# Down product of a gated block: the last eight of sixteen units as block products in two groups of four

## The chip, the cores and the metric

One NeuronCore of a Trainium2 chip runs the whole kernel. The metric is the device time of one execution in microseconds. Engines: TensorE (PE; PEld is its weight load), VectorE (DVE), ScalarE (ACT), GpSimd (POOL) and SyncE (SP), whose queue issues every DMA.

## The reference, cut to what matters

```
x = x + tanh(g_xattn) * attention(layernorm(x), ctx)        # x: 4 batches x 512 rows x 512
x = x + tanh(g_ffn) * ffn(layernorm(x))
ffn(x): up = x @ wu.T; gate = x @ wg.T                      # 2048 hidden, weights rounded to -1, 0, 1 times a scale
        hidden = silu(up) * gate
        return hidden @ wd.T
```

The change lies in the last line, `hidden @ wd.T`.

## The kernel before, in words

**Units.** The up and gate products are made in 16 units n: eight pairs of 128-wide blocks of the hidden dimension, for batches 0 and 1 (n = 0 to 7), and again for batches 2 and 3 (n = 8 to 15). In a unit the two batches and the two hidden blocks form a 2 x 2 scheme, and seven products (Strassen's, in Winograd's form) stand for eight: `product1` to `product7`, of 8 matmuls with 512 columns each (a high and a low f16 part of x, L692 and L694). Products 1, 6, 7 and 4 gather in `ps_c[n % 2]`, product 2 in `ps_y`, products 5 and 3 in `ps_z`. ScalarE copies partial results out (`copy_1`, `copy_5`, `copy_u2`), VectorE adds the others (`add_11`, `add_12`, `add_22`), and each waits for the other.

**Hidden parts.** A unit leaves four hidden blocks "11", "12", "21", "22" of 128 x 512: first index the hidden block, second the batch. ScalarE makes the SiLU (L1027), VectorE multiplies by the gate (`make_h`, L1342), ScalarE rounds to a high f16 part (`high_h`, L1033), VectorE subtracts for the low part (`low_h`, L1347).

**Down product.** For units 0 to 11 (`down_half`, L770): during unit n = 3 to 14 one down half stands between product 3 and product 7. It takes two finished units and one batch, 4 row tiles x 8 matmuls with 512 columns (L764), two PSUM halves in turn, and VectorE adds each tile to its rows (`evict`, L1382). For units 12 to 15 the down product is itself done by seven block products (`final`, L796 to L847) over 256-column halves: they need sums S1 to S4 of the hidden blocks (GpSimd L553 to L573, VectorE for unit 15 at L1466; high parts `high_s`, L1039; low parts `low_s`, L551 and L1352) and sums T1 to T4 of the down weights (GpSimd, L539 to L544). Parts 1, 6, 7, 4 and 5, 3 add up in their banks, so a part waits for the eviction of the one before. This is the kernel's tail, 224 matmuls of 256 columns (L806), evicted at L1395.

**Order.** Each engine's order is written out by hand and waits on semaphores. TensorE in unit n (L783): product 6, product 3, the down half, product 7, then products 1, 2 and 5 of unit n + 1, then product 4 of n. Product 6 waits for `copy_1`, product 3 for `copy_5`, product 7 for `copy_u2`, product 4 for `add_22`, product 2 and 5 of the next unit for `add_11` and `add_12`. ScalarE's queue is at L1102, VectorE's at L1400, GpSimd's at L531 to L573.

**Reload.** Rows of batches 0 and 1 are stored during units 9 and 10, and the rows of batches 2 and 3 are read back into the same buffer (L422); `shift` (L1073) adds a term to them on ScalarE.

Of the kernel before, what the change touches and what calls it, by code (L numbers as in the profile page):

```python
# [6 lines left out]
def gated_block_kernel(nc, x, xT, first, ctxT, wqkT, wugT, wdT, x1_dram, out):  # L7

# [35 lines left out]
    with stack:  # L44
# [109 lines left out]
        LAST_D = NN - 4  # L154
        FIN = [(j, t) for j in (1, 6, 5, 7, 2, 3, 4) for t in range(NT)]
# [88 lines left out]
        def sum_part(n, c, lo):  # L244

            if c == "S1":
                return h_part(n, "12", lo)
            k = ((n - LAST_D) * 3 + SUMS.index(c) - 1) * 2 + lo
            for home, size in ((xt_flat, 8), (xf[:, 6144:8192], 8), (t3_flat, 4), (early, 4)):
                if k < size:  # L250
                    return home[:, k * 256:(k + 1) * 256].bitcast(F16)
                k -= size

        def hidden(n, c, lo):
            return h_part(n, c, lo) if c in HSLOT else sum_part(n, c, lo)

        def hidden_ready(n, c):
            return (s_lo[c], n + 1) if c in HSLOT else (s_slo[c], n - LAST_D + 1)

        def last_td(r, c):  # L260

            view = t_d[:, 8 * DM:16 * DM].rearrange("p (u r c n) -> p u r c n", u=4, r=2, c=2)
            return view[:, :, r, c, :]

        def last_t(blk):

            m, u = {"T1": (0, 0), "T2": (0, 4), "T3": (1, 0), "T4": (1, 4)}[blk]
            units = wbf[:, m, :].rearrange("p (u c) -> p u c", u=NU)
            return units[:, u:u + 4, A21 * 256:(A21 + 1) * 256]

        def fin_done(j, t):

            return FIN.index((j, t)) + 1

        def fin_bank(j, t):

            if j in (1, 6, 7, 4):
# [23 lines left out]
        def _(sp):  # L301
# [122 lines left out]
            for b, t, j in ((2, 0, 3), (2, 1, 3), (2, 2, 3), (2, 3, 3), (3, 0, 4), (3, 1, 4), (3, 2, 4)):  # L424
                sp.wait_ge(s_ef, fin_done(j, t))
                sp.dma_start(out[b, t * P:(t + 1) * P, :], y_tile(b, t)).then_inc(d_out, 16)
            for c in (1, 0):
                sp.wait_ge(s_ef, fin_done((4, 7)[c], 3))
# [6 lines left out]
        def _(pool):  # L435
# [100 lines left out]
            hold(pool, s_tda, 3)  # L536
            hold(pool, d_tb["T3"], d_tb_done(NU, "T3"))
            hold(pool, s_sum, 4 * NU)
            pool.tensor_tensor(last_t("T1"), last_td(0, 1), last_td(0, 0), ALU.subtract).then_inc(s_tw, 1)  # L539
            pool.tensor_tensor(last_t("T3"), last_td(1, 1), last_td(0, 1), ALU.subtract).then_inc(s_tw, 1)  # L540
            hold(pool, s_tw, 1)
            pool.tensor_tensor(last_t("T2"), last_td(1, 1), last_t("T1"), ALU.subtract).then_inc(s_tw, 1)
            hold(pool, s_tw, 3)
            pool.tensor_tensor(last_t("T4"), last_td(1, 0), last_t("T2"), ALU.subtract).then_inc(s_tw, 1)  # L544
# [4 lines left out]
            def low_s(n, c):  # L549
                hold(pool, s_shi[c], n - LAST_D + 1)  # L550
                pool.tensor_tensor(sum_part(n, c, 1), sum_f32(c), sum_part(n, c, 0), ALU.subtract).then_inc(s_slo[c], 1)  # L551

            for k in range(3):  # L553
                n = LAST_D + k
# [18 lines left out]
                low_s(n, "S4")  # L573


        @block.tensor
        def _(pe):
# [120 lines left out]
            def product1(n):  # L698
# [11 lines left out]
                if n >= 4:  # L710
                    pe.wait_ge(s_ev, 4 * min(n - 3, LAST_D))
# [71 lines left out]
            for n in range(NN - 1):  # L783
# [9 lines left out]
            n = NN - 1  # L793
            ends = (NN - 4, NN - 3, NN - 2)

            def final(j, t, units, first, last):  # L796

                c, w = OPERAND[j], WEIGHT[j]
                if t == 0:
                    ready, count = hidden_ready(units[-1], c)  # L800
                    pe.wait_ge(ready, count)
                for u in units:
                    cols = last_t(w)[:, u - LAST_D, :] if j >= 4 else last_td(*w)[:, u - LAST_D, :] if j < 3 else \
                        last_td(1, 1)[:, u - LAST_D, :]
# [742 lines left out]
```

## Time and profile before

| | |
|---|---|
| median of 3 runs | 403.47 us (402.99 to 403.74) |
| the profiled execution | 402.79 us |
| its span, first to last instruction | 401.0 us |
| TensorE / VectorE / ScalarE / GpSimd busy | 395.7 / 295.3 / 261.2 / 127.0 us |
| TensorE clock granted, mean | 0.999 |

A row of a timeline is: start, duration, engine, line, operation, output and input, count, and in brackets the idle time before it and who ended it. A matmul's duration is its latency: matmuls follow each other sooner than that, so distances between starts are read. A row of a group is: line, engine, operation, forms, count, busy us, mean ns of one, idle time before.

### The profile page before, as it was taken

What the parts mean: (1) busy time and instruction counts of PE and PEld (TensorE: products, weight loads), DVE (VectorE), ACT (ScalarE), POOL (GpSimd) and SP (SyncE); (2) the same over time, 40 slices, a digit from 0 to 9 for tenths busy, and PEclk for the clock granted to TensorE, in tenths of its full rate; (3) what the DMA queues carried; (4) which work ended last, traced back from release to release, by engine and by line L of the source; (5) the groups of instructions that cost most, each with busy time, mean ns of one, the idle gap of its engine ahead of it and who ended that gap; (6) DMA issues with size and microseconds to landing.
All of it is one profiled execution on the core that took longest, in us unless ns stands there. A gap on an engine that the chain in (4) does not pass through costs nothing.

```text
span 401.0 us, 5690 instructions
## 1 busy us (share of the span) xinstructions
PE 395.7 (99%) x1816; PEld 197.6 (49%) x1816; DVE 295.3 (74%) x431; ACT 261.2 (65%) x349; POOL 127.0 (32%) x169
## 2 busy tenths in 40 slices
PE   8999999999999999999999999999999999999996
PEld 6545555454444444444444444444444444444785
DVE  0576578988899984879798877656565657595985
ACT  3886898889767786769788855733534556627510
POOL 0234254658865013313246004500000152525100
PEclk9999999999999999999999999999999999999999
DMA  8999939498600020020009533051400000000005
GB/s 306 412 418 401 386 117 235 137 284 188 159 0 3 0 105 2 0 106 0 1 16 226 111 65 60 26 183 54 158 0 2 0 2 1 0 2 1 2 2 209
DMA packets 42029, 43.89 MB, mean 109 GB/s; under 512 B 30864, under 2 KB 31120, under 8 KB 39952
## 3 DMA queue, kind: packets, MB, share of 16 engines
q1 hardware_dynamic: 42000, 43.53, 34.4%
q8 instruction: 15, 0.25, 0.2%
q14 instruction: 14, 0.11, 0.1%
HBM read 29.89 MB, written 6.29 MB: 90 GB/s over the span
## 4 chain that ended last, share of the span: by engine, by line
PE 82%; DVE 6%; ACT 5%; issue 4%; DMA 2%; SPq 1%; DVEq 0%; POOL 0%; ACTq 0%; POOLq 0%
PE pair L692 20%; PE pair L694 20%; PE pair L764 20%; PE pair L621 8%; PE pair L806 6%; PE pair L596 3%; PE pair L582 3%; DMA xf<-in_wdT 2%; PE pair L607 1%; ACT xf L1027 1%; ACT sh L1033 1%; DVE sh L1347 1%; DVE x_sb L1218 1%; PE pair L632 1%; DVE small L1223 1%
## 5 line engine op out<-in xcount | busy, mean ns | idle before, releaser
L692 PE MATMUL pair<-xb_hi,w_sb 128*128 128x512 f16 x448 | 169.8, 379 | 0.6 <-ACT xf L1071 0.3
L694 PE MATMUL pair<-xb_lo,w_sb 128*128 128x512 f16 x448 | 169.8, 379 | 0.0
L764 PE MATMUL pair<-x_sb,sh 128*128 128x512 bf16 x384 | 85.3, 379 | 0.3 <-DVE x_sb L1382 0.3
L692 PEld LDWEIGHTS pair<-xb_hi,w_sb 128*128 128x128 bf16 x448 | 43.8, 98 | 55.1 <-issue 1.5
L694 PEld LDWEIGHTS pair<-xb_lo,w_sb 128*128 128x128 bf16 x448 | 43.8, 98 | 52.3 <-issue 0.3
L1027 ACT ACTIVATE xf<-xf,small 128x512 f32<-128x512 f32 x48 | 34.6, 721 | 53.0 <-DVE xf L1337 31.2
L764 PEld LDWEIGHTS pair<-x_sb,sh 128*128 128x128 f16 x384 | 37.3, 98 | 46.5 <-DVE x_sb L1382 1.8
L621 PE MATMUL pair<-sh,xt_sb 128*128 128x512 f32 (+2 forms) x160 | 57.4, 508 | 0.0
L1342 DVE SCALAR_TENSOR_TENSOR xf<-xf,small 128x512 f32<-128x512 f32 x48 | 39.3, 821 | 12.2 <-ACT xf L1027 12.2
L1382 DVE SCALAR_TENSOR_TENSOR x_sb<-pair,small,x_sb 128x512 f32<-128x512 f32 x48 | 35.9, 747 | 13.4 <-PE pair L764 13.2
L621 PEld LDWEIGHTS pair<-sh,xt_sb 128*128 128x128 f32 x160 | 28.0, 190 | 26.2 <-issue 22.0
L1347 DVE TENSOR_TENSOR sh<-xf,sh 128x512 f16<-128x512 f32 x44 | 37.5, 858 | 0.4 <-ACT sh L1033 0.3
L1033 ACT ACTIVATE sh<-xf 128x512 f16<-128x512 f32 x44 | 27.1, 624 | 16.4 <-PE pair L764 10.7
L478 POOL TENSOR_TENSOR w_sb<-w_sb 128x512 bf16<-128x512 bf16 x8 | 9.6, 1196 | 65.2 <-ACT w_sb L899 65.2
L1332 DVE TENSOR_TENSOR xf<-pair,xf 128x1024 f32<-128x1024 f32 x16 | 19.6, 1222 | 13.8 <-PE pair L694 13.8
L1342 DVE SCALAR_TENSOR_TENSOR c<-c,small,pair 128x512 f32<-128x512 f32 x16 | 11.9, 745 | 18.2 <-ACT c L1027 18.2
L1059 ACT ACTIVATE xf<-pair 128x1024 f32<-128x1024 f32 x16 | 16.4, 1023 | 11.5 <-PE pair L694 11.3
L1327 DVE TENSOR_TENSOR xf<-pair,xf 128x1024 f32<-128x1024 f32 x16 | 19.5, 1221 | 4.9 <-PE pair L694 4.3
L558 POOL TENSOR_TENSOR xf<-xf 128x512 f32<-128x512 f32 x3 | 3.8, 1266 | 61.0 <-DVE xf L1342 61.0
L1337 DVE TENSOR_TENSOR xf<-pair,xf 128x1024 f32<-128x1024 f32 x16 | 19.5, 1220 | 3.9 <-PE pair L694 3.8
L1218 DVE SCALAR_TENSOR_TENSOR x_sb<-pair,small,x_sb 128x512 f32<-128x512 f32 x16 | 12.0, 747 | 11.8 <-PE pair L621 11.8
L893 ACT ACTIVATE w_sb<-w_sb,small 128x1024 f32<-128x1024 f32 x16 | 18.9, 1229 | 0.0
(151 smaller groups left out, 538.6 us busy)
## 6 DMA issues: line engine op xcount, KB each, us to landing
w_sb<-in_wugT SPq DMA_DIRECT2D x8, 1024.0 KB, 10.6
xt_sb<-in_xT SPq DMA_DIRECT2D x16, 256.0 KB, 5.1
x_sb<-in_x SPq DMA_DIRECT2D x4, 1024.0 KB, 9.5
xf<-in_wdT SPq DMA_DIRECT2D x4, 1024.0 KB, 6.4
xt_sb<-in_wdT SPq DMA_DIRECT2D x4, 1024.0 KB, 5.2
out<-x_sb SPq DMA_DIRECT2D x15, 256.0 KB, 2.0
x_dram<-x_sb SPq DMA_DIRECT2D x8, 256.0 KB, 2.8
x_sb<-x_dram SPq DMA_DIRECT2D x2, 1024.0 KB, 5.6
```

The source lines that it names most:

```text
L621: last = pe.matmul(ps_x[i % 2][:, lo:hi], xt_tile(i)[:, k, :], at[:, k, lo:hi], start=(k == 0), stop=(k == KD - 1))
L692: pe.matmul(dst[:, m * 512:(m + 1) * 512], w[:, o:o + P], hi[:, k], start=start and k == 0, stop=False, skip_group_check=not start)
L694: last = pe.matmul(dst[:, m * 512:(m + 1) * 512], w[:, o:o + P], lo[:, k], start=False, stop=k == 1, skip_group_check=not start)
L764: ins = pe.matmul(dst, h_part(n, c, lo)[:, i * P:(i + 1) * P], t_d[:, e * DM + lo_col:e * DM + hi_col], start=first and n == units[0] and ...
L806: ins = pe.matmul(fin_bank(j, t), hidden(u, c, lo)[:, t * P:(t + 1) * P], cols, start=first and u == units[0] and lo == 0 and (t % 2 == 0 ...
L1027: act.activation(cb(n, c)[:, 0:512], src, ACT.Silu, scale=su[:, :]).then_inc(s_silu[c], 1)
L1033: act.activation(h_part(n, c, 0), cb(n, c)[:, 0:512], ACT.Copy).then_inc(s_hi[c], 1)
L1327: dve.tensor_tensor(cb(n, "11"), ps_y[:, :], cb(n, "11"), ALU.add).then_inc(s_c["11"], 1)
L1332: dve.tensor_tensor(cb(n, "12"), ps_z[:, :], cb(n, "12"), ALU.add).then_inc(s_c["12"], 1)
L1342: dve.scalar_tensor_tensor(cb(n, c)[:, 0:512], cb(n, c)[:, 0:512], kap[:, :], gate, ALU.mult, ALU.mult).then_inc(s_mul[c], 1)
L1347: dve.tensor_tensor(h_part(n, c, 1), cb(n, c)[:, 0:512], h_part(n, c, 0), ALU.subtract)\
L1382: dve.scalar_tensor_tensor(y_tile(b, i), at, c_out[:, :], y_tile(b, i), ALU.mult, ALU.add)\
```

## The change

Units 8 to 11 are taken out of the down halves and become a first group (g = 0) of block products; units 12 to 15 stay the second group (g = 1).

- TensorE: down halves stand only in units 3 to 10. In each of units 12 to 15, row tile t = n - 12 of group 0 is worked off: seven parts (`between`) of 8 matmuls with 256 columns stand between the seven products, in two banks of the `ps_c` that the unit doesn't use. Unit 11 has no down work; its order is products 6, 3, 7, then 2 of unit 12, 4, then 1 and 5 of unit 12.
- The order of products in units 13 to 15 is 2, 5, 1, two parts, 6, 3, two parts, 7, two parts, 4, one part. In the tail the parts with block 1 of all four units stand in one piece.
- Sums S1 to S4 with high and low parts are now made for units 8 to 15. "12" has no part of its own from unit 8 on. New places for them: the weight units that are no longer read (`freed`) and, for units 14 and 15, the columns of the tile that is already used.
- GpSimd: T sums for both groups, two after unit 8, two after unit 9, two after unit 12, two after unit 13. It waits for all transposes of the second half before its first S3.
- ScalarE: the shifts of batches 2 and 3 go from units 12 and 13 to units 11 to 14, one tile of each; `sign_down(3)` stands a little earlier in unit 8. The queues of ScalarE and VectorE for units 11 to 15 are written anew.

The core of the diff:

```diff
-        LAST_D = NN - 4
-        FIN = [(j, t) for j in (1, 6, 5, 7, 2, 3, 4) for t in range(NT)]
+        G0, G1 = NU, NU + 4
+        PART = (1, 5, 6, 3, 7, 2, 4)
+        FIN = [(0, j, t) for t in range(NT) for j in PART] + [(1, j, t) for j in (1, 6, 5, 7, 2, 3, 4) for t in range(NT)]
...
+            if g == 0:
+                o = 0 if j in (1, 6, 7, 4) else 512
+                return ps_c[(t + 1) % 2][:, o:o + 256]
...
+                if n == G0:
+                    hold(pool, s_tda, 3)
+                    hold(pool, s_p[4], G0 + 1)
+                    weights_1(0)
+                if n == G0 + 1:
+                    weights_2(0)
+                if n == G1:
+                    hold(pool, s_p[4], G0 + 2)
+                    weights_1(1)
+                if n == G1 + 1:
+                    weights_2(1)
...
-            for n in range(NN - 1):
+            for n in range(G1 - 1):
                 product6(n)
                 product3(n)
                 if n >= 3:
                     down_half(n)
...
+            def between(n, j):
+
+                t = n - G1
+                if j in (1, 5):
+                    pe.wait_ge(s_mul["21"], n)
+                else:
+                    pe.wait_ge(s_ef, fin_done(0, {6: 1, 7: 6, 4: 7, 3: 5, 2: 3}[j], t))
+                final(0, j, t, group, j in (1, 5, 2), True)
+
+            n = G1 - 1
             product6(n)
             product3(n)
             product7(n)
...
+            product2(n + 1)
             product4(n)
+            product1(n + 1)
+            product5(n + 1)
+            for n in range(G1, NN):
+                if n == G1:
+                    product6(n)
+                    between(n, 1)
+                    product3(n)
+                    between(n, 5)
+                    between(n, 6)
+                    product7(n)
+                    between(n, 3)
+                else:
+                    product2(n)
+                    product5(n)
+                    product1(n)
+                    between(n, 1)
+                    between(n, 5)
+                    product6(n)
+                    product3(n)
+                    between(n, 6)
+                    between(n, 3)
+                    product7(n)
+                between(n, 7)
+                if n == G1:
+                    product4(n)
+                    between(n, 2)
+                else:
+                    between(n, 2)
+                    product4(n)
+                between(n, 4)
...
+            n = G1 - 1
+            silu(n - 1, "21")
+            copy_u2(n)
+            high_s(n - 1, "S1")
+            high_s(n - 1, "S2")
+            high_h(n - 1, "21")
+            silu(n, "12")
+            high_h(n, "11")
+            high_s(n - 1, "S4")
+            silu(n, "22")
+            high_s(n, "S3")
+            high_h(n, "22")
+            silu(n, "21")
+            copy_1(n + 1)
+            high_s(n, "S1")
+            high_s(n, "S2")
+            copy_5(n + 1)
...
+                else:
+                    silu(n - 1, "21")
+                    high_s(n - 1, "S1")
+                    high_h(n - 1, "21")
+                    high_s(n - 1, "S2")
+                    copy_5(n)
+                    high_s(n - 1, "S4")
+                    copy_1(n)
+                    silu(n, "11")
...
+            n = G1 - 1
             make_h(n - 1, "21")
             make_h(n, "11")
             add_12(n)
             low_h(n - 1, "21")
-            low_h(n, "11")
             add_22(n)
             make_h(n, "12")
             low_s(n - 1, "S1")
+            low_s(n - 1, "S2")
             make_h(n, "22")
+            low_h(n, "11")
+            low_h(n, "22")
+            make_h(n, "21")
+            add_11(n + 1)
+            low_s(n, "S1")
+            low_s(n, "S2")
+            low_h(n, "21")
```

## Rows read from the trace of the kernel before

**Rows 1.** The page, busy time of each engine and its share.
```profile
PE 395.7 (99%) x1816; PEld 197.6 (49%) x1816; DVE 295.3 (74%) x431; ACT 261.2 (65%) x349; POOL 127.0 (32%) x169
```

**Rows 2.** Units 8-11, 12-14: us, busy of PE, PEld, DVE, ACT, POOL, clock, DMA share, GB/s.
```profile
232.90:308.90 76.00, 76.00 (x354) 34.42 (x352) 48.62 (x61) 36.12 (x49) 9.83 (x4) 1.00 0.22 69
308.90:366.40 57.50, 57.18 (x265) 25.77 (x264) 39.68 (x46) 31.89 (x47) 21.18 (x16) 1.00 0.00 1
```

**Rows 3.** TensorE in order of time: down halves of units 12 and 14, product 7.
```profile
312.38 7.07 PE L764 MATMUL pair<-x_sb,sh 128*128 128x512 bf16 x32
319.29 0.38 PE L692 MATMUL pair<-xb_hi,w_sb 128*128 128x512 f16 x1
...
350.37 5.34 PE L764 MATMUL pair<-x_sb,sh 128*128 128x512 bf16 x24
356.03 1.90 PE L764 MATMUL pair<-x_sb,sh 128*128 128x512 bf16 x8 [0.32 <-DVE x_sb L1382]
357.77 0.38 PE L692 MATMUL pair<-xb_hi,w_sb 128*128 128x512 f16 x1
```

**Rows 4.** The tail: chain that ended last (start, us); weight loads by line.
```profile
376.96 20.97 PE pair L806 x192
...
L806 PEld LDWEIGHTS pair<-w_sb,sh 128*128 128x128 f16 x63 | 6.2, 98 | 0.8
```

**Rows 5.** VectorE and GpSimd in order of time, unit 14's down half.
```profile
353.67 1.64 DVE L1342 SCALAR_TENSOR_TENSOR xf<-xf,small 128x512 f32<-128x512 f32 x1
...
355.90 1.43 DVE L1352 TENSOR_TENSOR sh<-xf,sh 128x512 f16<-128x512 f32 x1
...
353.31 1.45 POOL L551 TENSOR_TENSOR xf<-xf 128x512 f16<-128x512 f32 x1 [2.87 <-ACT xf L1039]
355.52 1.26 POOL L558 TENSOR_TENSOR xf<-xf 128x512 f32<-128x512 f32 x1 [0.75 <-DVE xf L1342]
```

**Rows 6.** In order of time: unit 13 on GpSimd and VectorE, and a weight sum.
```profile
336.77 1.16 POOL L551 TENSOR_TENSOR xt_sb<-xf,xt_sb 128x512 f16<-128x512 f32 x1 [5.32 <-ACT xt_sb L1039]
...
334.68 0.74 DVE L1342 SCALAR_TENSOR_TENSOR xf<-xf,small 128x512 f32<-128x512 f32 x1
...
246.36 2.12 POOL L539 TENSOR_TENSOR w_sb<-x_sb 128x1024 bf16<-128x1024 bf16 x1 [29.46 <-ACT x_sb L1091]
```

**Rows 7.** VectorE by line and form: units 12 to 14, and the 256-column evictions.
```profile
L1347 DVE TENSOR_TENSOR sh<-xf,sh 128x512 f16<-128x512 f32 x6 | 6.5, 1076 | 0.0
L1352 DVE TENSOR_TENSOR xt_sb<-xf,xt_sb 128x512 f16<-128x512 f32 x2 | 1.4, 680 | 0.0
...
L1395 DVE SCALAR_TENSOR_TENSOR x_sb<-pair,small,x_sb 128x256 f32<-128x256 f32 x28 | 11.9, 476 | 3.5 <-PE pair L806 3.5
```

**Rows 8.** ScalarE by line and form, from 200 us on: a high part.
```profile
L1039 ACT ACTIVATE xt_sb<-xf 128x512 f16<-128x512 f32 x4 | 2.5, 620 | 0.8 <-POOL xf L558 0.8
```

**Rows 9.** SyncE's issues (start, us of issue), and from the page the landing times.
```profile
241.93 1.34 SPq L380 DMA_TRANSPOSE xb_lo<-xf  x1
...
284.40 0.38 SPq L422 DMA_DIRECT2D x_sb<-x_dram  x1
...
x_sb<-x_dram SPq DMA_DIRECT2D x2, 1024.0 KB, 5.6
...
xb_lo<-xf SPq DMA_TRANSPOSE x5, 3.3
```

**Rows 10.** Handovers in order of time: ScalarE, TensorE and VectorE.
```profile
125.74 1.00 ACT L1071 ACTIVATE xf<-pair 128x1024 f32<-128x1024 f32 x1
...
126.80 0.39 PE L692 MATMUL pair<-xb_hi,w_sb 128*128 128x512 f16 x1 [0.27 <-ACT xf L1071]
...
368.13 0.38 PE L692 MATMUL pair<-xb_hi,w_sb 128*128 128x512 f16 x1
...
368.33 1.02 ACT L1059 ACTIVATE xf<-pair 128x1024 f32<-128x1024 f32 x1 [1.04 <-PE pair L694]
...
321.31 1.23 DVE L1337 TENSOR_TENSOR xf<-pair,xf 128x1024 f32<-128x1024 f32 x1 [1.07 <-PE pair L694]
```

More of the change, by code:

```diff
@@ L792, in _, with final @@
                 product4(n)
-            n = NN - 1
-            ends = (NN - 4, NN - 3, NN - 2)
-            def final(j, t, units, first, last):
+            def final(g, j, t, units, first, last):
                 c, w = OPERAND[j], WEIGHT[j]
@@ L810, in final @@
                     ins.then_inc(s_fin, 1)
+            group = tuple(range(G0, G1))
+            def between(n, j):
[6 more added lines that the diff above has]
+            n = G1 - 1
             product6(n)
@@ L1101, in _ @@
             silu(0, "11")
-            for n in range(NN):
+            for n in range(G1 - 1):
                 down = n >= 3
@@ L1373, in evict @@
                     hold(dve, s_coef, 2)
-                if 32 <= k < 40 and i == 0:
-                    hold(dve, d_re[b % 2], 16)
                 if 16 <= k < 20:
@@ L1399, in _ @@
             weight_scale(2, 3, ps_pt[0], 3)
-            for n in range(NN - 1):
+            for n in range(G1 - 1):
                 down = 3 <= n
@@ L1463, in _ @@
                     ternary_down(2)
+            n = G1 - 1
+            make_h(n - 1, "21")
+            make_h(n, "11")
+            add_12(n)
+            low_h(n - 1, "21")
+            add_22(n)
+            make_h(n, "12")
+            low_s(n - 1, "S1")
+            low_s(n - 1, "S2")
+            make_h(n, "22")
+            low_h(n, "11")
[5 more added lines that the diff above has]
+            low_h(n, "21")
+            for n in range(G1, NN - 1):
+                t = n - G1
+                if n > G1:
+                    make_h(n - 1, "21")
+                    final_evict(0, 4, t - 1)
+                    low_s(n - 1, "S1")
+                    low_h(n - 1, "21")
+                    low_s(n - 1, "S2")
+                    add_11(n)
+                final_evict(0, 1, t)
+                make_h(n, "11")
+                if n > G1:
+                    final_evict(0, 5, t)
+                add_12(n)
+                if n == G1:
+                    final_evict(0, 5, t)
+                final_evict(0, 6, t)
+                if n > G1:
+                    final_evict(0, 3, t)
+                make_h(n, "12")
+                add_22(n)
+                if n == G1:
+                    final_evict(0, 3, t)
+                low_h(n, "11")
+                final_evict(0, 7, t)
+                make_h(n, "22")
+                final_evict(0, 2, t)
+                low_h(n, "22")
             n = NN - 1
             def last_sum(c, a, b, op):
-                hold(dve, s_slo[c], 3)
+                hold(dve, s_slo[c], 7)
                 dve.tensor_tensor(sum_f32(c), a, b, op).then_inc(s_sh[c], 1)
```

294 lines of the change are left out of this document (170 added, 124 removed), and 4 rows, old and new, of the table PLACE.

## The prediction

> **What bounds the kernel now.** I read the share of busy time first, then the stages, then TensorE's rows in order of time, and last the other three engines where TensorE's next work waits for them. TensorE is busy 395.7 of 401.0 us [rows 1], and in the stretch that the change touches (units 8 to 15) it is busy without a gap but for one [rows 2]: its clock is granted at 1.00, the full 2.4 GHz level, so no time is to be had there from the clock. The reader is to see that TensorE's own columns set the time, and that VectorE, ScalarE and GpSimd (40, 32 and 21 us busy in the 57.5 us of units 12 to 14) only matter where one of them hands over too late. A row of the chain of waits names what such a handover costs: in unit 14 the down product stops before its fourth tile for an eviction [rows 3]. Unit 12's 32 matmuls take 319.29 - 312.38 = 6.91 us, unit 14's take 357.77 - 350.37 = 7.40, so that wait costs 0.49 us (the row's own 0.32 counts only from the modelled end of the matmul before it).
>
> **Part 1, columns removed.** Four down halves go: 4 x 6.91 = 27.64 us. In their place stand 7 products x 4 row tiles x 8 matmuls of 256 columns = 224. The kernel has 192 such matmuls in a row at its end in 20.97 us, 0.1092 each [rows 4], so 224 take 24.46 us. Gain 27.64 - 24.46 = 3.18 us, all of it on TensorE, which is the bound. No product of the expansion is added or dropped. A 512-wide matmul paces at 6.91 / 32 = 0.216 and a 256-wide one at half of it, so the weight load of 98 ns is hidden behind either [rows 4].
>
> **A rule against the change.** The load rows of 98 ns stand inside a pace of 109.2 ns with only 11 ns to spare [rows 4]. The Trainium skill, "TensorE: Matmul & The Clock Gate", "The mechanism" (under "Part 3: Packing small matmuls — row/col tiling"), says a weight load overlaps running matmuls only when it is for another row group; here every load takes all rows. By that rule a load would stand ahead of each matmul; the rows above contradict it, and its result is among the rivals.
>
> **Part 2, the wait of 0.49 us.** Its cause is in unit 14: the multiply at 353.67 takes 1.64 us and the subtraction at 355.90 takes 1.43, where the same forms take 0.74 and 0.68 without a GpSimd operation beside them; each ends 0.55 us after the GpSimd operation it meets (353.31 + 1.45 = 354.76 to 355.31; 355.52 + 1.26 = 356.78 to 357.33) [rows 5 to 7]. So a VectorE operation with both inputs in SBUF waits for GpSimd's running one, and evictions and adds that read PSUM do not. This stays: unit 10 of the new order has the same queues as unit 14 had. I cost it at no change, between 0 and 0.6.
>
> **Part 3, more work on the other engines.** Units 8 to 11 now form S1 to S4 as 12 to 15 do: for each unit four sums and two low parts on GpSimd (1.27 and 1.16 us each [rows 5, 6]), two low parts more on VectorE (0.68, [rows 7]) and three high parts more on ScalarE (0.62, [rows 8]). Off the path in themselves. VectorE gets 28 evictions of 0.48 us for 16 of 0.75 (13.4 for 12.0 us). GpSimd's wait for the last transpose is free: it is issued at 241.93 and lands some 3.3 us later [rows 9]; the sum S3 of unit 8 moves from 240.5 to 245.3, its high part on ScalarE ends at 247.2, and the copy of product 1 behind it ends near 249, 3 us before product 6 wants it. The two reloads of x1 (issued at 284.40 at the latest, 5.6 us to land [rows 9]) are there long before the shifts at about 307. ScalarE's sign pass of the down weights moves within unit 8 to a place where four shifts of 0.6 us stood in unit 12 at no cost.
>
> **Part 4, the four weight sums on GpSimd.** They ran in one piece where GpSimd was free. Now two stand in its queue after unit 8's last low part and two after unit 9's. One takes 2.12 us [rows 6]. What is queued behind is S3 of the next unit, and ScalarE's queue stops at S3's high part: behind that stand the SiLU of 22, the copy of product 1, high 22, the SiLU of 11 and the copy of product 5. Worked out on unit 13's rows, which unit 9 repeats: low S4 ends at 337.93 [rows 6]; + 4.2 for the two sums + 0.5 for VectorE's S2 between them = 342.6; S3 to 343.9; ScalarE: high 0.5, SiLU 0.6 to 345.0, copy of product 1 to 346.0; add_11 on VectorE to 347.3; SiLU 11 to 348.0; copy of product 5 to 349.05. Product 3 would start at 348.6. Stall 0.4 us (bounds 0 and 1.0: without, and with one more meeting of 0.55). In unit 10 the same pair starts 2.5 us sooner, since no shifts are queued on ScalarE, and costs nothing.
>
> **Part 5, the changeover from unit 11 to 12.** Here the order is new, and no long down product covers the other engines. Times from product 6 of unit 11, products of 1.73 us: product 7 ends at 5.2, product 4 runs 6.9 to 8.6, product 1 of unit 12 to 10.4, product 5 to 12.1, then product 6 must find the copy of product 1. ScalarE: copy of product 6 to 2.9, three high parts to 4.5, SiLU 12 (after add_12, 3.7 to 5.0) to 5.7, high 11 to 6.25, high S4 of unit 10 to 6.8. GpSimd: low S4 6.9 to 8.4. VectorE: add_22 to 6.7, multiply 12 to 7.35, then low S1 must wait for GpSimd's 8.4 and ends at 9.0; GpSimd's S3 then waits for it and ends at 10.2; low S2 waits for that and ends at 10.7; multiply 22 to 11.4. ScalarE: high 22 to 12.0, SiLU 21 to 12.6, copy of product 1 to 13.6. ScalarE to TensorE takes 0.06 us (125.74 + 1.00 to 126.80 [rows 10]), so product 6 starts at 13.65 in place of 12.1: stall 1.55 us. The backlog goes on through unit 12: copy of product 5 behind high S2 0.3, eviction 1 behind two low parts 0.2, copy of product 6 0.1, and add_22 behind the SiLU and multiply of 12, which wait for the late copy of product 6: 0.6. Together 2.75 us; bounds 0 (no meeting of VectorE and GpSimd: VectorE would be 2.2 sooner, which clears it) and 4.
>
> **Part 6, short covers in units 12 to 15.** Two places now have only two block parts, 16 x 0.1092 = 1.75 us, as cover. Copy of product 1: it starts 0.20 us after the product ends, as the copy at 368.33 does where product 3 follows product 6 at 368.13 [rows 10], takes 1.00 and is seen 0.06 later, 1.26: 0.49 to spare, but high S4 of the unit before stands ahead of it in ScalarE's queue and ends about then. I take 0.05 in each of units 13 to 15, 0.15 in all (bounds 0 and 1.5). Add_22: 0.29 after the product (319.29 + 8 x 0.216 = 321.02 to 321.31 [rows 3, 10]), 1.23, 0.06 = 1.58: 0.17 to spare, free when VectorE is idle by then, which it is from unit 13 on. A hidden chain for block parts (part 6 waits for eviction 1, and so on) has over 1 us in hand: 0.20 + 0.48 + 0.06 = 0.74 for an eviction [rows 7].
>
> **Part 7, the tail.** The last group keeps its 224 matmuls. Product 4 of unit 15 is now followed by one part more (0.87) and all of block 1, so the SiLU and sums of 21 have 4.3 us more cover than before. 0.
>
> **The sum.** -3.18 + 0 + 0.4 + 2.75 + 0.15 = +0.12 us. On the profiled execution's own time (402.79, span 401.0) this is 402.9; the median of the runs shown, 403.47, lies 0.68 higher, and I forecast on it: **403.6 us**. 0.2% of this is 0.8 us, about what a measurement can tell from no change.
>
> **The sharing rule.** The rows show an operation held back by the whole of the other's [rows 5]. The Trainium skill, "SBUF — State Buffer", "Who interferes with whom", says a VectorE instruction with two SBUF inputs and a GpSimd instruction that reads SBUF exclude each other for the whole instruction, and that the one issued second waits. By that rule, the trace agrees; were it not so, the changeover's 2.75 us would go, to the time of rival 1.
>
> **The rivals.** (1) *The meetings fall otherwise and the gain is kept.* VectorE and GpSimd meet or miss by 0.1 or 0.2 us; if low S1 of unit 10 gets ahead of low S4 on GpSimd (7.3 against 6.9), VectorE meets GpSimd once in place of twice, is 1.6 us sooner, and the changeover costs 0 to 1. For it: the difference is 0.4 us. Against: in units 12 to 14 the low parts of 21, 11 and 22 from the f32 buffers (L1347) take 1076 ns in the mean over six where 680 is free [rows 7], so meetings are the rule where both queues are full. Time 403.6 - 2.75 = 400.9, down to 403.47 - 3.18 - 0.49 = 399.8. (2) *Slower: GpSimd's chain holds the copy of product 1 in every unit.* S1, S2, low S3 and S4 follow each other on GpSimd, and high S4 stands ahead of the copy. If each of the four meets a VectorE operation (1.6 in place of 1.2, as L551's 1.45 and more), high S4 ends 0.5 us later in units 12 to 15: 4 x 0.5 = +2.0, 405.6. It decides from 0.05 us of lateness on, since my layout has nothing in hand there. (3) *Loads not hidden*: 224 x 0.098 = 22 us, 425; the 192 matmuls of the tail speak against it. (4) *The change doesn't do what it says* (the parts leave as much time idle as the down halves took because VectorE evicts late): 403.47 + 3.2 = 406.7; evictions are 28 x 0.48 us in the 72 us of four units, so little speaks for it.
>
> **How the numbers follow.** Forecast case 0.45, all of it within 0.8 us; rival 1 0.29 (faster); rival 2 0.24, rivals 3 and 4 0.01 each (slower), with 0.01 of rival 2 falling inside 0.8. So faster 0.29, same 0.46, slower 0.25. The range reaches from the near end of rival 1, 401.0 (part of its cases, 0.10, lies below), to rival 2's 405.6 (0.10 above). The forecast's own range is 402.8 to 404.4.
>
> **What would show it.** Right: in TensorE's rows, 256-wide matmuls at a pace of 109 ns between products; idle before product 6 of unit 12 of 1 to 2 us, released by ScalarE's copy of product 1; idle before product 3 of unit 10; VectorE subtractions of 1.3 to 1.8 us on GpSimd's ends in units 10 to 12. Wrong: no idle time at the changeover and 3 us less between product 6 of unit 8 and the last matmul (rival 1); idle before product 6 in each of units 13 to 15 (rival 2); idle in the tail (part 7).

## The result and the profile of the changed kernel

The changed kernel takes 404.53 us (median; 403.89 to 405.21), the kernel before 403.06 (402.75 to 403.74) in runs beside it: ratio 1.0034, 95% interval 1.0022 to 1.0047. The time lies in the predicted range and 0.9 us above the predicted one, but the case is another: I had forecast +0.12 us, no change within 0.2%, and the kernel is 1.47 us (0.34%) slower than the kernel before in the runs beside it, whose median is now 0.41 us lower than the one that I had forecast on. The profiled execution took 404.20 us, span 402.3; before 402.79 and 401.0. So 1.4 us are to be found, 1.3 of them in the span.

The page of the changed kernel, busy time of each engine; it answers to [rows 1].

```profile
PE 393.6 (98%) x1904; PEld 206.3 (51%) x1912; DVE 308.2 (77%) x447; ACT 267.5 (66%) x361; POOL 171.4 (43%) x197
```

TensorE is busy 2.1 us less than in [rows 1], GpSimd 44 us more. Two stretches of the changed part, from unit 8's down product to the last matmul: us, busy PE, PEld, DVE, ACT, POOL, granted clock, DMA share, GB/s; they answer to [rows 2].

```profile
236.83:312.00 75.17, 73.16 (x345) 33.47 (x347) 55.68 (x63) 43.20 (x65) 43.66 (x28) 1.00 0.21 67
312.00:398.17 86.17, 85.76 (x606) 58.71 (x604) 69.50 (x106) 38.72 (x57) 34.95 (x22) 1.00 0.04 13
```

Together 161.34 us. The same stretch of the kernel before runs from 236.41 to 397.77: 161.36. (Both ends are counted by the pace, start to start, not by the modelled ends.) The clock was granted at 1.00 in both, and what the removed columns gave was idle time again, as forecast. TensorE in order of time at the three longest waits that are new:

```profile
272.87 0.38 PE L732 MATMUL pair<-xb_lo,w_sb 128*128 128x512 f16 x1
273.49 0.39 PE L730 MATMUL pair<-xb_hi,w_sb 128*128 128x512 f16 x1 [0.24 <-ACT xf L1158]
...
303.13 0.38 PE L732 MATMUL pair<-xb_lo,w_sb 128*128 128x512 f16 x1
304.74 0.39 PE L730 MATMUL pair<-xb_hi,w_sb 128*128 128x512 f16 x1 [1.23 <-ACT xf L1136]
...
314.62 0.38 PE L847 MATMUL pair<-w_sb,early 128*128 128x256 bf16 x2
315.42 0.39 PE L730 MATMUL pair<-xb_hi,w_sb 128*128 128x512 f16 x1 [0.41 <-DVE xf L1468]
```

A wait is read against the pace: 304.74 - 303.13 - 0.216 = 1.39 us before product 6 of unit 12 (the row's own 1.23 starts at the modelled end). In the same way 0.40 before product 3 of unit 10 and 315.42 - 314.62 - 2 x 0.1092 = 0.58 before product 4 of unit 12. L1158 is the copy of product 5, L1136 that of product 1, L1468 add_22.

Why the copy is late is on VectorE and GpSimd in order of time, just before it: L1483 are the low parts of S1 and S2 of unit 10, L576 on GpSimd the low part of S4, L585 the difference S3 of unit 11. They answer to [rows 5].

```profile
298.55 1.65 DVE L1483 TENSOR_TENSOR sh<-xf,sh 128x512 f16<-128x512 f32 x1
300.12 1.75 DVE L1483 TENSOR_TENSOR xf<-xf 128x512 f16<-128x512 f32 x1
301.79 0.74 DVE L1473 SCALAR_TENSOR_TENSOR xf<-xf,small 128x512 f32<-128x512 f32 x1
...
298.18 1.47 POOL L576 TENSOR_TENSOR t_sb<-xf,t_sb 128x512 f16<-128x512 f32 x1 [3.36 <-ACT t_sb L1126]
299.61 1.71 POOL L585 TENSOR_TENSOR xf<-xf 128x512 f32<-128x512 f32 x1
```

Each of the two VectorE operations ends 0.55 us after the GpSimd operation beside it (300.20 after 299.65, 301.87 after 301.32), as in [rows 5]. It is the same all through this trace: from 230 us on, 19 VectorE operations of 512 columns that read no PSUM take over 0.9 us, and each of them ends 0.55 us after a GpSimd operation.

Where, then, are the 1.3 us of span? At the two ends, outside what the change touches. The last eviction of the kernel before and of the changed one:

```profile
397.96 0.48 DVE L1395 SCALAR_TENSOR_TENSOR x_sb<-pair,small,x_sb 128x256 f32<-128x256 f32 x1 [0.39 <-PE pair L806]
```

```profile
398.37 0.48 DVE L1524 SCALAR_TENSOR_TENSOR x_sb<-pair,small,x_sb 128x256 f32<-128x256 f32 x1 [0.39 <-PE pair L847]
```

It is over at 398.44 and at 398.85, 0.41 later. That much was lost in the first 7 us; from there on the two kernels take the same time to it. The second row of the f32 projections, in the kernel before and in the changed one.

```profile
5.94 1.89 PE L642 MATMUL pair<-xf 128*128 128x256 f32 x8
```

```profile
6.34 1.89 PE L680 MATMUL pair<-xf 128*128 128x256 f32 x8
```

From the last eviction to the end of the span it is 401.0 - 398.44 = 2.56 us before and 402.3 - 398.85 = 3.45 after: 0.89 more, where the code is the same. SyncE's issues of the last nine stores (start, us), and the line of the first seven (duration of an issue, min/median/max, and the time to landing); first the kernel before.

```profile
393.33 4.60 SPq L426 DMA_DIRECT2D out<-x_sb  x7
397.98 0.94 SPq L429 DMA_DIRECT2D out<-x_sb  x2
```

```profile
L426 SPq DMA_DIRECT2D out<-x_sb x7: 332/333/460, 393.3 to 397.6; - x7
DMA to landing us min/median/max: 2.0/2.3/2.6
```

The changed kernel:

```profile
393.74 4.74 SPq L451 DMA_DIRECT2D out<-x_sb  x7
398.52 1.27 SPq L454 DMA_DIRECT2D out<-x_sb  x2
```

```profile
L451 SPq DMA_DIRECT2D out<-x_sb x7: 332/432/1116, 393.7 to 398.0; - x7
DMA to landing us min/median/max: 2.3/3.0/3.3
```

One issue takes 1.12 us in place of at most 0.46, and the stores land in 3.0 us in place of 2.3. The DMA queues of the changed kernel between 394 and 397 us show what is among them:

```profile
q1 hardware_dynamic: 405, 0.75, 67.3%
q8 instruction: 1, 0.02, 2.1%
```

One packet of 16 KB of the instruction queue, at 395.6. The kernel before has none there; its last two fall at 373.9 and 388.1.

### The profile page after: what moved, and what is told of

It is laid out like the page before. It is cut to its first block, busy times and chain, and to the rows that moved or that the text cites. A ratio compares the mean times of both kernels' runs of the same rounds, so it can differ in the third digit from the quotient of the medians.

```text
span 402.3 us, 5933 instructions
## 1 busy us (share of the span) xinstructions
PE 393.6 (98%) x1904; PEld 206.3 (51%) x1912; DVE 308.2 (77%) x447; ACT 267.5 (66%) x361; POOL 171.4 (43%) x197
## 4 chain that ended last, share of the span: by engine, by line
PE 70%; DVE 10%; ACT 7%; issue 7%; POOL 2%; DMA 2%; SPq 1%; DVEq 0%; ACTq 0%; POOLq 0%
PE pair L730 16%; PE pair L732 16%; PE pair L847 11%; PE pair L804 11%; PE pair L659 8%; PE pair L634 3%; PE pair L620 3%; DVE sh L1478 2%; DMA xf<-in_wdT 2%; PE pair L645 1%; ACT xf L1109 1%; DVE xf L1463 1%; DVE xf L1473 1%; ACT x_sb L1166 1%; ACT sh L1120 1%
## 5 line engine op out<-in xcount | busy, mean ns | idle before, releaser
L804 PE MATMUL pair<-x_sb,sh 128*128 128x512 bf16 x248 | 55.3, 379 | 0.8 <-DVE x_sb L1510 0.3
L804 PEld LDWEIGHTS pair<-x_sb,sh 128*128 128x128 f16 x256 | 24.7, 98 | 31.4 <-DVE x_sb L1510 1.8
L1478 DVE TENSOR_TENSOR sh<-xf,sh 128x512 f16<-128x512 f32 x36 | 30.7, 858 | 0.9 <-ACT sh L1120 0.8
L1524 DVE SCALAR_TENSOR_TENSOR x_sb<-pair,small,x_sb 128x256 f32<-128x256 f32 x56 | 25.2, 477 | 7.8 <-PE pair L847 7.4
L1510 DVE SCALAR_TENSOR_TENSOR x_sb<-pair,small,x_sb 128x512 f32<-128x512 f32 x32 | 23.8, 745 | 6.5 <-PE pair L804 6.4
L1120 ACT ACTIVATE sh<-xf 128x512 f16<-128x512 f32 x36 | 22.2, 625 | 7.0 <-DVE xf L1473 5.9
L585 POOL TENSOR_TENSOR xf<-xf 128x512 f32<-128x512 f32 x7 | 9.8, 1396 | 34.9 <-DMA xb_lo<-xf 28.6
L1468 DVE TENSOR_TENSOR xf<-pair,xf 128x1024 f32<-128x1024 f32 x16 | 19.5, 1218 | 3.3 <-PE pair L732 3.2
L1349 DVE SCALAR_TENSOR_TENSOR x_sb<-pair,small,x_sb 128x512 f32<-128x512 f32 x16 | 12.0, 747 | 11.8 <-PE pair L659 11.8
## 6 DMA issues: line engine op xcount, KB each, us to landing
w_sb<-in_wugT SPq DMA_DIRECT2D x8, 1024.0 KB, 10.6
```

What stands on the lines that cost most here:

```text
L804: ins = pe.matmul(dst, h_part(n, c, lo)[:, i * P:(i + 1) * P], t_d[:, e * DM + lo_col:e * DM + hi_col], start=first and n == units[0] and ...
L1120: act.activation(part(n, c, 0), shaped(n, c, cb(n, c)[:, 0:512]), ACT.Copy).then_inc(s_hi[c], 1)
L1478: dve.tensor_tensor(part(n, c, 1), shaped(n, c, cb(n, c)[:, 0:512]), part(n, c, 0), ALU.subtract)\
L1510: dve.scalar_tensor_tensor(y_tile(b, i), at, c_out[:, :], y_tile(b, i), ALU.mult, ALU.add)\
L1524: dve.scalar_tensor_tensor(fin_rows(j, t), fin_bank(g, j, t), c_out[:, :], fin_rows(j, t), ALU.mult, ALU.add).then_inc(s_ef, 1)
```

## The experiments

Two theories. **Theory G** is the forecast's own: TensorE's waits in units 10 to 12 come from GpSimd's queue and from VectorE operations that GpSimd's hold back. **Theory F** is new: the 0.89 us at the end is the instruction packet meeting the last stores, not the changed work. The rivals stand in each expectation.

**Is it there again?** The changed kernel once more, nothing edited.

> The changed kernel once more, for a second profile. In its first profile the stretch from unit 8's down product to the last matmul is as long as before (161.3 us), but the first projections end 0.4 us later and the time from the last eviction's end to the span's end is 3.45 us in place of 2.56. Theory F (an instruction fetch on the 16 DMA engines meets the last stores, since the longer TensorE program moves it there): the end is again 3.2 to 3.6 us, the first 0.4 us may be gone. Theory R (both are chance): the end is about 2.6 in this profile and the ratio to before about 1.000 to 1.001.

Measured: 404.52 us, ratio 1.0025 (1.0011 to 1.0039). Stalls 0.40, 0.48, 1.39, 0.23, 0.16, 0.13, 0.58 again, the packet 1.8 us after the first store's start, the end 3.31 us. The difference from the kernel before is 1.08 us here, 1.47 in the first result. Neither the stalls nor the end are chance.

**The packet moved off the stores, in the changed kernel.** The waits have long been met when TensorE comes to them; they lengthen its program by 112 instructions (the page counts 6045 in place of 5933: two of the waits become one instruction).

```
 def product(n, j, dst, a, blk, start):
...
+                if n < NU:
+                    for _ in range(4):
+                        pe.wait_ge(s_ones, 1)
```

> The changed kernel with 112 more semaphore instructions on TensorE's queue in units 0 to 7 (always satisfied), which bring the last fetch of TensorE's instructions about 6 us ahead, from 395.5 to about 389.5, clear of the stores from 393.7 on. Theory F: last eviction to end falls from 3.45 to 2.6 us, the kernel is 0.7 to 0.9 us faster than e1_after_again. Theory R: no difference, within 0.3 us.

Measured: 403.68 us, ratio 1.0009 (0.9997 to 1.0022), 0.84 us less than the run beside it without the waits; what is left against the kernel before, 0.24 us, is not clear of zero. The packet fell at 389.8, the end is 2.6; issues and landing of the stores are those of the kernel before:

```profile
L451 SPq DMA_DIRECT2D out<-x_sb x7: 332/333/448, 394.4 to 398.7; - x7
DMA to landing us min/median/max: 2.0/2.3/2.6
```

The stalls in units 10 to 12 stay. Against the first store the packet moved from 1.8 us behind to 4.6 ahead, 6.4 us for 112 instructions or 57 ns each, which is about half a 256-column matmul's 109 (a matmul and its load are two instructions). Only TensorE's program was edited, so it is this program that the packet reads in.

**The same waits in the kernel before**, with the same lines in its `product`.

> The kernel before with the same 112 instructions in the same places. Its last fetch in the span is at 388.0 and the next would be due near 402; now one falls near 396, among the stores. Theory F: its end grows from 2.56 to about 3.4 us, the kernel is 0.7 to 0.9 us slower than before (ratio about 1.002). Theory R: ratio 1.000 within 0.0007.

Measured: 403.89 us, ratio 1.0019 (1.0003 to 1.0035); end 2.58 us. No packet fell among the stores: one came at 382.0 and the next, one more than in the kernel before, at 403.0, 2.1 us behind the last instruction. My count of instructions was wrong, so on the stores this run tells only that without a packet among them the end is 2.6. Yet the kernel is 0.45 us slower, clear of zero. The time outside the span is 1.7 to 3.5 us in its twelve executions, where it is 1.7 to 1.9 in those with six and eight waits: a part of the loss lies behind or ahead of the program, and whether that late packet makes it was not tested. I then counted from the packets' own places.

**Six and eight waits in the kernel before.** 168 and 224 instructions more.

> The kernel before with six extra waits that are long met ahead of each block product of the first eight units. Theory F (one packet of the instruction queue among the last stores makes their issues longer and their landing later, about 0.8 us): with four such waits no packet stood there, since the program was too short for another one; with six it is long enough, and the packet falls at 393 to 394, where the last stores begin. End of the last eviction to the end of the span 3.2 to 3.5 us in place of 2.6, one of the store issues over 1 us; 0.7 to 1.0 us slower than the kernel before, 404.1 to 404.5. Rival (the longer end belongs to the changed kernel's own order of the work): the end stays at 2.6, time within 0.5 us of the kernel before. If the packet falls elsewhere than among the stores, the end stays at 2.6 by theory F too.

> The kernel before with eight such waits ahead of each product: the same extra packet, about 3 us earlier (390 to 391), ahead of the first of the last stores at 393.3. Theory F: the packet is there but meets no store, so the end is 2.6 us again and the time that of the kernel before plus at most 0.4 (the added waits themselves, as with four). Rival (any extra packet or the waits themselves cost the 0.8): as slow as with six waits.

Measured with six: 403.52 us, ratio 1.0006 (0.9996 to 1.0016); the packet falls at 393.7, 0.2 us behind the start of the first store. One issue took 1.07 us and the landing is 2.5, but the end is 2.66. The stores after it may have room to catch up; that is argued, not shown. The forecast of 0.7 to 1.0 us failed; a packet that meets the first store costs 0.1, which the medians can't tell from nothing. Measured with eight: 403.03 us, ratio 0.9989 (0.9978 to 1.0000); packet at 391.5, end 2.53. An extra packet ahead of the stores costs nothing, nor do 224 more instructions.

**The packet placed as in the changed kernel, in the kernel before.** 133 instructions.

```
+                if n < 7:
+                    for _ in range(6 if n < 6 else 2):
+                        pe.wait_ge(s_ones, 1)
```

> The kernel before with six extra met waits ahead of each product of units 0 to 5 and two ahead of those of unit 6: 35 instructions of TensorE's program fewer than with six in all eight, so that the last packet of the instruction queue falls 1.9 us later against the stores: at 1.7 to 2.0 us behind the start of the first of the last stores, where it falls in the changed kernel (there 1.9 behind), instead of at the first store itself. Theory F: the end is 3.2 to 3.5 us in place of 2.6, the landings of the stores 2.9 to 3.1 in place of 2.3, both issues of the last block 1.27 in all in place of 0.95, and the kernel is 0.7 to 0.9 us slower than the kernel before with its waits: 404.1 to 404.5 (ratio 1.0015 to 1.003). Rival (the longer end belongs to the changed kernel's own work): 2.5 to 2.7, and 403.2 to 403.9.

Measured: 404.47 us against 403.25, ratio 1.0028 (1.0016 to 1.0041). The packet fell at 395.2, 1.7 us behind the first store's start. SyncE's issues and the first line of stores:

```profile
393.51 5.05 SPq L426 DMA_DIRECT2D out<-x_sb  x7
398.61 1.25 SPq L429 DMA_DIRECT2D out<-x_sb  x2
```

```profile
L426 SPq DMA_DIRECT2D out<-x_sb x7: 332/432/1452, 393.5 to 398.1; - x7
DMA to landing us min/median/max: 2.1/3.1/3.6
```

The last eviction ends at 398.62 and the span at 402.4: 3.78 us. The kernel before, with none of the change in it, has the changed kernel's long end and its time. The run with six waits differs from it by 35 such instructions and so in where the packet falls. That settles theory F; the size was over my 3.2 to 3.5. All 14 profiles bear it out, whatever the kernel: the seven with the packet 1.7 to 1.9 us behind the first store's start have an end of 3.25 to 3.8 us, the six without a packet among the stores one of 2.5 to 2.6, and the one at 0.2 us has 2.66.

**Theory G: the weight sums one unit later on GpSimd.**

```
-                if n == G0:
+                if n == G0 + 1:
...
                     weights_1(0)
-                if n == G0 + 1:
+                if n == G0 + 2:
                     weights_2(0)
```

> The changed kernel with the weight sums of the first four units one unit later on GpSimd: T1 and T3 behind the work of unit 9 in place of unit 8, T2 and T4 behind unit 10 in place of unit 9. Theory G (GpSimd's queue is the one that has no room): 2 x 2.6 us now stand between the sums of unit 10 and the difference h11-h12 (S3) of unit 11, for which the copy of product 1 of unit 12 waits on ScalarE. The 0.40 before product 3 of unit 10 goes; the 1.39 before product 6 of unit 12 grows to about 5.9, the 0.23, 0.16 and 0.13 behind it go; sum +3.5 us against the changed kernel, 407.5 to 408.5. Rival (GpSimd has room, 43% busy, and the changeover stall is made by the order of ScalarE's own queue): the stall at product 6 stays at 1.4 and the kernel is 0.4 faster, 404.1.

Measured: 409.91 us against 403.24, ratio 1.0152 (1.0124 to 1.0180). The 0.40 went, the wait before product 6 of unit 12 is 5.75. In time order, GpSimd's two weight sums ahead of S3, and TensorE behind the copy that waits for S3:

```profile
300.06 2.57 POOL L567 TENSOR_TENSOR w_sb<-x_sb,w_sb 128x1024 bf16<-128x1024 bf16 x1
302.78 2.38 POOL L569 TENSOR_TENSOR w_sb<-x_sb,w_sb 128x1024 bf16<-128x1024 bf16 x1
305.12 1.70 POOL L585 TENSOR_TENSOR xf<-xf 128x512 f32<-128x512 f32 x1
...
303.58 0.38 PE L732 MATMUL pair<-xb_lo,w_sb 128*128 128x512 f16 x1
309.55 0.61 PE L730 MATMUL pair<-xb_hi,w_sb 128*128 128x512 f16 x1 [5.59 <-ACT xf L1136]
309.95 0.63 PE L732 MATMUL pair<-xb_lo,w_sb 128*128 128x512 f16 x1
```

The rival is out: GpSimd is busy 43% of the span and has no room here. 5.75 in place of 1.39 + 0.23 + 0.16 + 0.13 + 0.40 is 3.4 us, as expected; but from unit 8's down product to the last matmul the kernel lost 6.0 (5.4 between the medians, over my 407.5 to 408.5; its four executions lie in two pairs 2.3 us apart, and the trace is of the longer one). The stretches around that wait (columns as above) show most of the rest:

```profile
304.00:309.50 5.50, 0.00 (x0) 0.00 (x0) 4.76 (x4) 2.64 (x5) 5.50 (x4) 0.82 0.00 0
309.50:312.94 3.44, 3.39 (x9) 1.16 (x9) 3.44 (x4) 3.25 (x6) 3.44 (x3) 0.50 0.00 0
```

After the idle 5.5 us the clock is granted at 0.50, the 1.2 GHz level: product 6's eight matmuls take 312.94 - 309.55 = 3.39 us in place of 1.73, and the block part behind it takes 1.55 in place of 0.87, 2.3 us lost together. New waits of 0.48 and 0.45 in units 13 and 14 stand against the 0.58 before product 4, which went. No shorter wait of any run here did that.

**The weight sums spread**, each pair right behind S3 of units 9 and 10 instead of behind the low parts of S4 of units 8 and 9.

> The changed kernel with T1 and T3 of the first four units put behind S3 of unit 9 and T2 and T4 behind S3 of unit 10 on GpSimd. Theory G: the high part of S3(9) no longer stands behind 2 x 2.6 us, so copy 5 of unit 10 comes in time: the 0.40 before product 3 of unit 10 is gone, nothing else moves (1.39, 0.23, 0.16, 0.13, 0.58 at the changeover and 0.48 in the down half stay), so -0.35 us against the changed kernel, 404.1 to 404.2. Rival (the 0.40 comes from ScalarE's four shifts of unit 9): it stays, time as the changed kernel.

Measured: 404.11 us, ratio 1.0020 (1.0011 to 1.0030). That is 0.87 us over the kernel before in the runs beside it, where the changed kernel was 1.08 over it: the medians are too coarse for 0.4 us, the trace decides. The 0.40 is gone and 0.48, 1.39, 0.23, 0.16, 0.13, 0.58 stand. That stall was the two sums ahead of S3, not the shifts.

**Two GpSimd operations made short.** They work on 32 of their 512 columns; the rest of both results is left out.

```
-                pool.tensor_tensor(part(n, c, 1), sum_f32(c), part(n, c, 0), ALU.subtract).then_inc(s_slo[c], 1)
+                w = 32 if n == G1 - 2 and c == "S4" else 512
+                pool.tensor_tensor(part(n, c, 1)[:, 0:w], sum_f32(c)[:, 0:w], part(n, c, 0)[:, 0:w],
+                                   ALU.subtract).then_inc(s_slo[c], 1)
...
-                pool.tensor_tensor(sum_f32("S3"), h_of(n, "11"), h_of(n, "12"), ALU.subtract).then_inc(s_sh["S3"], 1)
+                w = 32 if n == G1 - 1 else 512
+                pool.tensor_tensor(sum_f32("S3")[:, 0:w], h_of(n, "11")[:, 0:w], h_of(n, "12")[:, 0:w],
+                                   ALU.subtract).then_inc(s_sh["S3"], 1)
```

> The changed kernel with two GpSimd operations over 32 columns in place of 512: the low part of S4 of unit 10 and the difference S3 of unit 11 (the rest of both is left out, so the output is that of wrong hidden parts). Theory G (the chain of GpSimd operations, met by VectorE's, holds the copy of product 1 of unit 12): about 2.2 us of GpSimd work is gone ahead of the copy; the stalls 1.39, 0.23, 0.16 and 0.13 vanish, the 0.58 before product 4 stays (it is ScalarE's and VectorE's own order), as do 0.40 and 0.48 in unit 10: the stretch from unit 8's down half to the last product is 1.9 to 2.1 us shorter than in the changed kernel. Rival (the copy waits for its place on ScalarE behind the silu of block 21 and two high parts): the 1.39 shrinks by less than 0.5.

Measured: 402.97 us in a single execution, span 401.1. The same five operations as in the changed kernel's fence:

```profile
299.36 0.73 DVE L1487 TENSOR_TENSOR sh<-xf,sh 128x512 f16<-128x512 f32 x1
300.01 0.73 DVE L1487 TENSOR_TENSOR xf<-xf 128x512 f16<-128x512 f32 x1
300.67 0.74 DVE L1477 SCALAR_TENSOR_TENSOR xf<-xf,small 128x512 f32<-128x512 f32 x1
...
298.99 0.56 POOL L577 TENSOR_TENSOR t_sb<-xf,t_sb 128x32 f16<-128x32 f32 x1 [3.37 <-ACT t_sb L1130]
299.64 0.56 POOL L588 TENSOR_TENSOR xf<-xf 128x32 f32<-128x32 f32 x1
```

VectorE's two subtractions take 0.73 us in place of 1.65 and 1.75. 1.39, 0.23, 0.16 and 0.13 are gone; 0.41, 0.48 and 0.58 stay. The stretch from unit 8's down product to the last matmul is 1.92 us shorter than in the unedited run. The changeover stall comes from these two GpSimd operations: 2.06 us of their own (1.47 and 1.71 down to 0.56 each) and what VectorE loses where it meets them. This run doesn't part the two; the next keeps every operation and moves only the order.

**Can the meetings be ordered away?** First ScalarE's and VectorE's queues of units 11 and 12 alone, every operation kept. The core of it, VectorE's queue in unit 11 and then ScalarE's:

```
             n = G1 - 1
+            make_h(n, "11")
             make_h(n - 1, "21")
-            make_h(n, "11")
             add_12(n)
-            low_h(n - 1, "21")
             add_22(n)
-            make_h(n, "12")
             low_s(n - 1, "S1")
-            low_s(n - 1, "S2")
+            low_h(n - 1, "21")
+            make_h(n, "12")
             make_h(n, "22")
             low_h(n, "11")
-            low_h(n, "22")
             make_h(n, "21")
+            low_s(n - 1, "S2")
+            low_h(n, "22")
...
```

```
             n = G1 - 1
...
+            high_s(n - 1, "S4")
             silu(n, "12")
-            high_h(n, "11")
-            high_s(n - 1, "S4")
             silu(n, "22")
-            high_s(n, "S3")
-            high_h(n, "22")
+            high_h(n, "11")
             silu(n, "21")
+            high_h(n, "22")
+            high_s(n, "S3")
             copy_1(n + 1)
```

> The changed kernel with the queues of ScalarE and VectorE in units 11 and 12 in another order (sums' low parts after the multiplies, copies of products 1, 5 and 6 ahead of the high parts of the sums). Theory of the changeover: the idle times before product 6, product 3, product 7 and product 4 of unit 12 and before part 6 (2.5 us in the trace) go, those of unit 10 (0.40 and 0.48) stay; 2.3 to 2.9 us faster than e1_after_again, ratio to before 0.996 to 0.998. Rival (TensorE waits there because the new order of products leaves two blocks of cover, not because of what is queued): still over 1 us idle at product 6 or product 4 of unit 12.

Measured: 402.92 us, ratio 0.9982 (0.9969 to 0.9995), 1.60 us less than the changed kernel beside it, where I had expected 2.3 to 2.9. All waits of the changeover are gone, and one that I had not laid out stands in unit 13:

```profile
319.49 0.38 PE L732 MATMUL pair<-xb_lo,w_sb 128*128 128x512 f16 x1
320.61 0.38 PE L730 MATMUL pair<-xb_hi,w_sb 128*128 128x512 f16 x1 [0.74 <-DVE x_sb L1529]
```

0.90 us for part 4's eviction, queued behind two low parts that met GpSimd; that is the missing part of the gain. The packet met the stores here too (end 3.25).

**Everything mended at once**: that order with the low part of block 22 of unit 12 moved behind unit 13's eviction of part 6, the spread weight sums, in unit 10 `evict_half(n, 1)` ahead of `make_h(n, "12")`, and the four waits that move the packet.

> The changed kernel with four things at once: the other order of ScalarE's and VectorE's queues in units 11 and 12 as in the reordered kernel, but the low part of block 22 of unit 12 moved behind the first evictions of unit 13 (so that part 4's eviction no longer waits for it); the weight sums behind S3 of units 9 and 10; in unit 10 the eviction of the down half's second tile ahead of block 12's product of silu; and the four extra waits per product in the first eight units that move the instruction fetch off the last stores. Expected: no stall over 0.1 in units 8 to 12 (0.40, 0.48 and 0.90 gone), perhaps 0.5 before product 6 of unit 14, so the stretch to the last product is 2.9 to 3.5 us shorter than in the changed kernel, and the end 0.85 shorter: 400.4 to 401.2, 0.6% faster than the kernel before (ratio 0.993 to 0.996). If a meeting of VectorE and GpSimd falls otherwise than laid out, one stall of 0.5 to 1.0 us stands in unit 12 or 13: 401.2 to 402.2.

Measured: 401.61 us, ratio 0.9957 (0.9943 to 0.9972). No wait over 0.03 us in units 8 to 12, end 2.52; left are 0.48 in unit 13 and 0.86 before product 6 of unit 14, so it is nearer the second of the two cases that I gave. In unit 13 a multiply on VectorE took 2.70 us beside two weight sums on GpSimd.

**And the last two**, on GpSimd and, for units 13 to 15, on ScalarE.

```
             def weights_1(g):
                 pool.tensor_tensor(down_t(g, "T1"), down_td(g, 0, 1), down_td(g, 0, 0), ALU.subtract).then_inc(s_tw, 1)
+                if g == 1:
+                    hold(pool, s_mul["11"], G1 + 2)
...
                 copy_5(n)
-                high_s(n - 1, "S4")
                 copy_1(n)
+                high_s(n - 1, "S4")
```

> The best kernel so far with two orders mended: in units 13 to 15 ScalarE copies product 1 ahead of the high part of S4, and on GpSimd the sum T3 of the last four units waits until VectorE's product of silu of block 11 of unit 13 is done. Theory G (every stall left is a VectorE or ScalarE operation that a GpSimd operation holds): the 0.48 before part 5's neighbour in unit 13 (VectorE's product of silu lasted 2.70 us beside the 2 x 2.1 us of weight sums) and the 0.86 before product 6 of unit 14 both go: 1.3 us less, 400.1 to 400.5, ratio to the kernel before 0.992 to 0.994. Rival (they move to the next wait): within 0.4 of the best kernel so far, 401.2 to 401.7.

Measured: 400.51 us against 403.40, ratio 0.9936 (0.9918 to 0.9954): faster than both kernels. One row of the two stretches:

```profile
237.00:312.00 75.00, 74.84 (x365) 35.78 (x367) 56.80 (x67) 44.06 (x66) 44.36 (x29) 1.00 0.22 67
312.00:395.09 83.09, 83.00 (x587) 56.95 (x585) 69.15 (x102) 38.54 (x57) 33.11 (x22) 1.00 0.04 16
```

The stretch is 158.09 us, 3.27 less than the 161.36 of the kernel before: the 3.18 of the removed columns and its 0.49 of unit 14, less 0.36 of waits that are left (the longest 0.26), come to 3.31.

## Why the prediction was right and wrong

- **Columns removed** (part 1): right. The matmuls of the block parts pace at 109 ns, and busy TensorE fell. The trace disagrees again with the rule on weight loads, as the prediction said: the loads of 98 ns cost nothing at that pace.
- **The 0.49 us of unit 14** (part 2): right. It stands in unit 10 at 0.48, and is gone when the eviction is queued earlier.
- **Weight sums** (part 4): right, 0.40 forecast, 0.40 measured, and its cause shown by the spread sums. My bounds of 0 to 1.0 hold only for that place: one unit later the same four operations made the kernel 5.4 us slower.
- **The changeover** (part 5): right in place, cause and order, 2.75 forecast, 1.39 + 0.23 + 0.16 + 0.13 + 0.58 = 2.49 measured (1.55 was 1.39). Even the layout's times came out: from product 6 of unit 11 (291.26), low S4 ends at 8.4, low S1 at 8.9, S3 at 10.1, low S2 at 10.6, and product 6 of unit 12 starts at 13.5, where I had 8.4, 9.0, 10.2, 10.7 and 13.65. The runs with two short operations and with the other order show the cause for the first four. That 0.58 comes from the SiLU and multiply of block 12 is argued, not shown; other queue orders removed it.
- **Short covers** (part 6): 0.04, 0.07 and 0.08 where I took 0.05 each.
- **Work off the path** (part 3) and **the tail** (part 7) up to the last eviction: right, no other wait.
- **The sum** of these was +0.12 us; the stretch from unit 8's down product to the last matmul measured -0.02. That the time fell into 401.0 to 405.6 says little, since this range takes in most of the rivals; the single waits are what bears the mechanism out.
- **The step that failed** is part 7, "The tail ... 0". It looked at matmuls and evictions, and took what follows the last eviction as fixed. That end is 2.56 us before and 3.45 after, since the longer and shifted TensorE program puts an instruction packet among the last stores. Moving the packet away in the changed kernel gives 0.84 us back; putting it there in the kernel before costs 1.2. The 0.89 is the larger part of the 1.47 us between the medians. The profile's other 0.41, in the first 7 us, I take for chance: profiles of the kernel before with added waits differ there by up to 1.5 us (the second row of projections starts at 5.85 with four waits and at 7.34 with eight). With more executions the 1.47 became 1.08, of which 0.84 went with the packet.
- **Rival 1** (meetings fall otherwise, 399.8 to 400.9) did not happen by itself, but it is real: ordered away, the kernel takes 400.5. **Rival 2** (the copy late in every unit) did not: 0.04 to 0.08 in units 13 to 15. It came up in its mild form when I moved things, 0.86 in unit 14. **The sharing rule** of the Trainium skill ("SBUF — State Buffer", "Who interferes with whom"), by which a VectorE instruction with two SBUF inputs and a GpSimd one that reads SBUF exclude each other: the trace agrees, and the run with short operations shows it as a cause: 1.65 and 1.75 us back to 0.73.

## What to carry to other kernels

When an edit removes 3 us from the bounding engine and puts more work on the others, lay out the queues of all engines around it in order of time before costing it: here that gave each stall to 0.2 us, showed that GpSimd at 43% was full where it mattered, and later which orders give the 3 us back. Treat the stores behind the last result as part of the path, and look in the DMA queues for instruction packets among them whenever an edit changes the number of instructions: a difference of 0.2% can come from such a packet, and a few met waits ahead of products tell it from the change itself. Compare stretches between the same two instructions of both kernels before explaining a difference of medians.

## What the runs showed of the hardware

- One 16 KB instruction packet between the last stores lengthens one store issue to 0.9 to 1.5 us (at most 0.46 otherwise), the median landing from 2.3 to between 2.8 and 3.1 us and the last two issues from 0.95 to between 1.15 and 1.33 in all; the kernel ends 0.7 to 1.2 us later. At the first of these stores it costs 0.1, ahead of them nothing. Why the later issues and landings stay long is open.
- The packet's place follows TensorE's instruction count: 112 more instructions move it 6.4 us against the stores.
- After 5.5 us without a matmul the next two blocks of matmuls ran at a granted clock of 0.50, the 1.2 GHz level, and took 4.94 us in place of 2.60; after 1.4 us without one it stayed at 1.00.
- A VectorE operation with two SBUF inputs that meets GpSimd ends about 0.55 us after GpSimd's, also where GpSimd's is only 0.56 us long (299.55 to 300.09).
